# Feed-forward stage 3 of a four-layer block: gate and up products of both token halves interleaved over two banks

## The reference, cut to what matters

```python
def _matmul_lora(x, w, a, b, scale=1.0):
    out = jnp.einsum('bsd,hd->bsh', x, w)
    out = out + jnp.einsum('bsr,hr->bsh', jnp.einsum('bsd,rd->bsr', x, a), b) * scale
    return out
gate = _matmul_lora(x, gate_w, gate_a, gate_b)
up = _matmul_lora(x, up_w, up_a, up_b)
hidden = jax.nn.silu(gate) * up
out = _matmul_lora(hidden, down_w, down_a, down_b)
...
x = x + jnp.tanh(g_ffn[2]) * _L2_ffn_ref(_layernorm(x, axis=-1), ...)
```

## Time and profile before

| | before |
|---|---|
| median of 3 runs (lowest to highest) | 3038.99 us (3037.25 to 3041.05) |
| span of the profiled execution | 3039.3 us |
| TensorE (PE) busy, matmuls | 2869.5 us (94%), 14914 |
| weight loads (PEld) busy | 2371.4 us (78%), 14914 |
| VectorE (DVE) busy | 1945.8 us (64%) |
| ScalarE (ACT) busy | 1097.9 us (36%) |
| GpSimd (POOL) busy | 909.7 us (30%) |
| chain that ended last | PE 81%, DVE 11%, ACT 4%, issue 3% |

### The profile page before, as it was taken

How to read it: one execution, slowest core, us unless ns; L and a number is a source line. 1 busy time by engine, 2 the same in 40 slices (tenths; PEclk the granted TensorE clock), 3 DMA queues, 4 the chain that set the end, 5 groups by cost and what they waited for, 6 DMA issues and landing times.

```text
span 3039.3 us, 47992 instructions
## 1 busy us (share of the span) xinstructions
PE 2869.5 (94%) x14914; PEld 2371.4 (78%) x14914; DVE 1945.8 (64%) x4181; ACT 1097.9 (36%) x3288; POOL 909.7 (30%) x780
## 2 busy tenths in 40 slices
PE   7997799999999999898999999989999999999997
PEld 5665588888888887676888888868877888888886
DVE  5666765565566556575888888854462666666667
ACT  4654233333333333123444444421113444444442
POOL 5433043243334324222222222234442222222210
PEclk9998999999999999999999999999999999999999
DMA  3000011011111111011011101111111001001000
GB/s 128 15 4 18 20 46 40 27 52 38 35 41 41 38 31 46 25 32 35 29 28 32 32 28 28 29 35 52 53 49 45 25 26 29 25 26 29 25 8 28
DMA packets 55235, 104.40 MB, mean 34 GB/s; under 512 B 6672, under 2 KB 6928, under 8 KB 54928
## 3 DMA queue, kind: packets, MB, share of 16 engines
q1 hardware_dynamic: 51840, 94.39, 10.8%
q10 hardware_dynamic: 3216, 7.81, 0.7%
HBM read 100.09 MB, written 2.10 MB: 34 GB/s over the span
## 4 chain that ended last, share of the span: by engine, by line
PE 81%; DVE 11%; ACT 4%; issue 3%; ACTq 0%; DVEq 0%
PE proj L577 35%; PE outp L577 21%; PE score L577 12%; PE value L577 9%; PE turned L806 3%; ACT probs L1231 3%; DVE top L1585 1%; DVE x L1526 1%; DVE stats L1382 1%; DVE probs L1564 1%; DVE probs L1602 1%; DVE xt_lo L1411 1%; DVE sums L1596 0%; DVE probs L1406 0%; DVE vz L1478 0%
## 5 line engine op out<-in xcount | busy, mean ns | idle before, releaser
L526 POOL TENSOR_TENSOR w_hi<-raw,zero 128x512 fp32r<-128x512 f32 x352 | 377.5, 1072 | 1819.2 <-PE proj L577 638.8
L1526 DVE SCALAR_TENSOR_TENSOR x<-outp,gate,x 128x512 f32<-128x512 f32 x800 | 574.4, 744 | 53.8 <-PE outp L577 53.7
L530 POOL TENSOR_TENSOR w_lo<-raw,w_hi 128x512 fp32r<-128x512 f32 x352 | 467.2, 1327 | 27.6
L577 PE MATMUL proj<-xt_hi,w_lo 128*128 128x512 f32 x928 | 396.6, 427 | 9.3 <-DVE xt_lo L1411 4.8
L577 PE MATMUL outp<-w_hi,a_lo 128*128 128x512 f32 x800 | 334.8, 418 | 48.4 <-DVE a_lo L1634 25.2
L577 PE MATMUL proj<-xt_hi,w_hi 128*128 128x512 f32 x928 | 367.9, 396 | 0.0
L577 PE MATMUL proj<-xt_lo,w_hi 128*128 128x512 f32 x928 | 366.1, 394 | 0.0
L577 PE MATMUL outp<-w_hi,a_hi 128*128 128x512 f32 x800 | 317.8, 397 | 0.0
L577 PE MATMUL outp<-w_lo,a_hi 128*128 128x512 f32 x800 | 317.1, 396 | 0.0
L1101 ACT ACTIVATE pT<-turned 128x512 f32<-128x512 f32 x320 | 192.2, 601 | 292.4 <-PE turned L806 292.4
L1602 DVE TENSOR_TENSOR probs<-probs,inv 128x512 f32<-128x512 f32 x320 | 285.8, 893 | 8.8
(11 more groups left out here) (242 smaller groups left out, 5127.9 us busy)
## 6 DMA issues: line engine op xcount, KB each, us to landing
raw<-in_stream SPq DMA_DIRECT2D x352, 256.0 KB, 2.6
ctx_raw<-in_ctx_t ACTq DMA_DIRECT2D x4, 512.0 KB, 6.1
x<-in_x_in ACTq DMA_DIRECT2D x2, 1024.0 KB, 11.7
pb<-in_position_bias ACTq DMA_DIRECT2D x1, 2048.0 KB, 8.8
out<-x SPq DMA_DIRECT2D x8, 256.0 KB, 2.0
qw<-in_qweight ACTq DMA_DIRECT2D x1, 768.0 KB, 4.0
ln_w<-in_ln_weight ACTq DMA_DIRECT2D x1, 256.0 KB, 2.8
q_bi<-in_q_bias ACTq DMA_DIRECT2D x1, 256.0 KB, 2.6
```

Source lines behind the costliest of these rows:

```text
L526: pool.tensor_tensor(w_hi[:, k, :], raw[:, k % RAW, :], zero[:, :].to_broadcast([P, D]), ALU.add)\
L530: pool.tensor_tensor(w_lo[:, k, :], raw[:, k % RAW, :], f32(w_hi[:, k, :]), ALU.subtract)\
L577: m = pe.matmul(out_, l, r, start=start, stop=stop, skip_group_check=True)
L1526: dve.scalar_tensor_tensor(out=x[:, b, :], in0=O[no_f(k) % 2][:, :], scalar=g, in1=x[:, b, :], op0=ALU.mult, op1=ALU.add)\
```

## The change

`gate_or_up` no longer makes one half at a time. It is called with w (gate or up) and part (0 or 1). Each stationary tile is used for half 0 into J[w] and, right after it, for half 1 into S[w]. Part 0 holds the low-rank matmuls and the first two of the four tiles of width (16 matmuls), part 1 the other two (12). The down work is spread over the gaps behind the parts: behind gate part 0 nothing; behind gate part 1 `down_low` and tiles 0, 1, 2; behind up part 0 tiles 3, 4, 5; behind up part 1 tiles 6, 7. ScalarE makes both silus one after the other, VectorE adds tiles 0 to 5 of the down product and then makes `hidden` for both halves, and then adds tiles 6, 7. The number of matmuls, their shapes and operands are the same.

```diff
-                def gate_or_up(j, t, w):
-
-                    no = 2 * j + t
+                def gate_or_up(j, w, part):
+
                     lora, c = f_chunk(2, ("l", j)), f_chunk(2, ("gu"[w], j))
-                    if w == 0 and no >= 2:
-                        pe.wait_ge(s["hid"], no - 1)
-                    if j == 0:
-                        pe.wait_ge(s["low_lo"], t + 1)
-                    dst = (J if t == 0 else S)[w][:, :]
-                    stacked(dst, ring(lora, tokens(w)), M2["low"][:, half(t)], True, True, False)
-                    for kt in range(KT):
-                        last = kt == KT - 1
-                        m = mm3(dst, ring(c, tokens(kt)), acts("x", kt, half(t)), False, last, last)
-                    m.then_inc(s["proj"], 1)
-                    owed[0] += t
+                    dst = J[w][:, :], S[w][:, :]
+                    if part == 0:
+                        if j:
+                            pe.wait_ge(s["hid" if w else "silu"], 2 * j)
+                        else:
+                            pe.wait_ge(s["low_lo"], 2)
+                        for no, rows in enumerate(ring(lora, tokens(w))):
+                            for t in range(2):
+                                told(mm(dst[t], rows, M2["low"][:, half(t)], no == 0, False))
+                    for kt in (0, 1) if part == 0 else (2, 3):
+                        both = ring(c, tokens(kt))
+                        for no, (a, b) in enumerate(((1, 0), (0, 1), (0, 0))):
+                            done = kt == KT - 1 and no == 2
+                            for t in range(2):
+                                m = mm(dst[t], both[a], acts("x", kt, half(t))[b], False, done)
+                                if done:
+                                    m.then_inc(s["proj"], 1)
+                                else:
+                                    told(m)
+                    if w or not j:
+                        owed[0] += part
...
                 for j in range(HIDDEN_TILES):
-                    for no, (t, w) in enumerate(((0, 0), (0, 1), (1, 0), (1, 1))):
-                        gate_or_up(j, t, w)
-
-                        if j and no == 0:
+                    for no in range(4):
+                        gate_or_up(j, no // 2, no % 2)
+
+                        if j and no == 1:
                             down_low(j - 1)
-                        if j:
-                            down(j - 1, range(2 * no, 2 * no + 2))
+                            owed[0] += 1
+                        if j and no:
+                            down(j - 1, range(3 * no - 3, min(3 * no, B)))
...
-                        act.wait_ge(s["proj"], 2 + 2 * no + 1)
+                        act.wait_ge(s["proj"], 2 + 4 * j + t + 1)
...
-                        act.wait_ge(s["hid"], no + 1)
+                    for t in range(2):
+                        act.wait_ge(s["hid"], 2 * j + t + 1)
...
-                    dve.wait_ge(s["proj"], 2 + 2 * no + 2)
+                    dve.wait_ge(s["proj"], 2 + 4 * j + t + 3)
...
                     if j:
-                        add_tiles(j - 1, range(0, 2))
+                        add_tiles(j - 1, range(0, 6))
                     hidden(j, 0)
-                    if j:
-                        add_tiles(j - 1, range(2, 6))
                     hidden(j, 1)
```

## The result

| | before | the change |
|---|---|---|
| median (lowest to highest), 5 runs each | 3038.99 us (3037.25 to 3041.05) | 3052.52 us (3044.12 to 3053.32) |
| ratio | | 1.0035, 95% interval 1.002 to 1.005 |
| profiled execution | span 3039.3 us | time 3052.52 us, span 3049.9 us |
| F2, from its first gate matmul to L3's first matmul | 229.65 us | 239.44 us |
| behind F2, to the last matmul | 771.7 us | 771.3 us |

The change makes the kernel slower: 0.35% by the ratio of the runs, which is 10.6 us, and 13.5 us by the two medians; forecast were 13.3. The two spans differ by 10.6 us. Runs of one kernel scatter with their mean granted clock: of the change's five, the one at 0.988 had a span of 3041.4 us and the one at 0.982 had 3051.4.

A forecast was written before the change was run, and what follows sets the result against it. TensorE, waiting for nothing, was taken to bound F2: number of matmuls times spacing. Terms 1.6 + 8.2 + 1.7 + 1.8 = 13.3 us on the median of 3038.99 gave 3052.3 us, range 3045 to 3061.

The forecast's parts named there:

- Runs of three down tiles: In F2's periods, the third tile waits 0.41 us for VectorE to hand over its bank, 20 times: +8.2 us.
- Weight loads: In F2's gate and up matmuls, loads are already hidden, so using a stationary tile twice saves nothing: 0 us.
- Spacing: In F2's 616 gate and up matmuls, alternating banks gives the down run's 0.2333 us spacing: +1.6 us.
- Start: At j = 0 the first gate matmul must wait for low_lo of both halves: +1.7 us.
- Hidden chain inside the periods: In F2's periods, hidden of both halves starts later but is still ready before down_low needs it: 0 us.
- End: At j = 10 no gate work covers the hidden chain, taken with one slow hid_lo: +1.8 us, bounds 0.7 and 2.9.
- (b): Rival: shared tiles shorten the gate and up spacing, giving back 8.1 us: 3042.6 us, or 3046.7; chance 0.10.
- (c): Rival: faster than before, a tile's second matmul taking 0.173 us or less: 3033 us or less; chance 0.02.
- (d): Rival: the hidden chain becomes the bound, down_low waiting some 1 us in each of 10 periods: 3062 us; chance 0.06.
- (e): Rival: almost no cost, the O bank's hand-over being quicker in a run of three than at the end: 3044 us; chance 0.04.

The follow-up runs named there:

- e1_pairs: The change with down tiles in runs of two instead of three: 3050.84 us against 3041.09 for the kernel before, ratio 1.003.
- e2_threes: The kernel before with only its down tiles regrouped into runs of three, three and two, nothing interleaved: 3046.47 us, ratio 1.0024.
- e3_apart: The change with half 1 taking the width tiles in swapped order, so gate and up tiles are not used twice in a row: 3053.25 us, ratio 1.0037.
- e9_change_placed: The change plus 20 satisfied waits, so that L3's loop starts at instruction 11733 as in the kernel before: 3049.37 us, ratio 1.0029.
- e6_before_placed: The kernel before plus 176 satisfied waits (88 instructions) in F2, so that L3's loop starts at instruction 11821: 3046.34 us, ratio 1.0022.

## Why the prediction was right

The direction, the size and the main mechanism held; one smaller term had the wrong sign. Step by step:

- **Runs of three down tiles, forecast 8.2 us.** Right. The hand-over takes 1.58 us in the change as it did in the last run of before, and 18 loads wait in nine periods. By the periods a run of three costs 0.40 us (20.64 against 19.84 in e1_pairs, for two). e2_threes shows it alone (F2 + 7.9 us) and e1_pairs shows the change without it (F2 - 8.4 us).
- **Weight loads, forecast 0.** Right: e3_apart has the same F2 to 0.1 us with the sharing gone, and the 750 matmuls of the change's window have 749 loads. The Trainium skill (TensorE: Matmul & The Clock Gate, "What happens when you issue a matmul") says that one can load once and matmul repeatedly. No run here did that: each matmul brought its load along, so its gain was not put to the test.
- **Spacing, forecast +1.6 us.** The sign was wrong. With the runs of three gone, in e1_pairs, a period takes 19.84 us, against 19.87 in before: alternating the bank with each matmul costs nothing and rather gains a trifle, 0.3 us in ten periods. The step that failed was to take the down run's 0.2333 as the nearest row since it changes bank often. What makes the down run slower stays open; a change of bank by itself does not, as the interleaved products show (0.2275 to 0.2288 us each).
- **Start, forecast 1.7 us.** Right, in a row against the earlier trace rows:

```profile
2034.67 0.68 DVE L1824 TENSOR_TENSOR low<-score,low 32x512 fp32r<-32x512 f32 x1 [3.10 <-ACT low L1111]
...
2035.50 0.47 PE L577 MATMUL proj<-low,w_hi 128*128 128x512 f32 x1 [1.50 <-DVE low L1824]
```

  VectorE's instruction came 0.41 us earlier in this execution than in before, so the first matmul would have been at 2033.84: 1.66 us, and 0.08 for the longer first matmul.
- **Hidden chain inside the periods, forecast 0.** Right: `turned` waits for `hid_lo` only at the end, and the waits of the nine periods have no such row.
- **End, forecast 1.8 us.** The sum was right, its parts were not. The timeline of the change, against the earlier trace rows:

```profile
2253.20 0.39 PE L577 MATMUL score<-xt_hi,w_hi 128*128 128x512 f32 x1
...
2256.84 1.40 DVE L1837 TENSOR_TENSOR hid_lo<-hid,hid_hi 128x512 fp32r<-128x512 f32 x1 [0.70 <-ACT hid_hi L1111]
...
2258.38 0.77 PE L577 MATMUL value<-hid_hi,w_lo 128*128 128x512 f32 x1 [1.77 <-DVE hid_lo L1837]
...
2262.19 0.50 PE L577 MATMUL outp<-w_hi,hid_lo 128*128 128x512 f32 x1
```

  One `hid_lo` was slow (1.40 us, not 1.80), and `value` came 5.18 us behind the last up matmul, not 5.6, which makes 1.4 us. From there to the third tile it took 3.81 us, where before had 3.33: the granted clock had fallen, which the prediction did not reckon with, and the three `value` matmuls started 0.99 us apart from first to last, not 0.55. The end costs 8.99 - 7.12 = 1.9 us; that the two misses cancel is luck.

Start 1.7, ten periods at 0.78 each 7.8 and end 1.9 make 11.4 us, against 13.3 forecast and 13.5 by the medians; e9_change_placed, with more runs beside it, has 9.6 us. So the terms agree to 2 us, the misjudged spacing being most of the difference, and the match of the forecast with the first pair of medians to 0.2 us is luck. Of the rivals, (b) and (c) are refuted by e3_apart for this program, (d) by the waits, (e) by the hand-over's 1.58 us. What no rival had is the placement of L3's loop: the change itself moved it by 10 instructions only, which the stretch behind F2 does not show (771.3 against 771.7 us).

## What to carry to other kernels

On an engine that is busy all the time, ask first what a new order makes it wait for: here regrouping tiles from two to three on two banks cost 0.4 us twenty times, since the hand-over from a tile to the tile after next takes longer (1.58 us to its second matmul) than the matmuls in that stretch (1.17 us). The price could be read before the change in the one place where the same run already stood. Reusing a tile saves nothing while each matmul still brings a load that is hidden behind the matmul before. And before two orders are compared by the clock of the whole program, compare the stage itself: instructions added to one stage can move a later loop and cost as much as the effect that is looked for.

## What the runs showed of the hardware

- The place of a loop in TensorE's program matters. With L3's loop starting at instruction 11733 (or 11723), the weight loads of its first score matmuls wait about 3 us once at each of the two turns; with the start at 11821 they wait 2.2 to 3.6 us a second time, two matmuls later. e6_before_placed is 6.6 us slower with nothing else changed. That these are waits for instructions is a guess from the profile's "issue", which names no releaser; which placements are good was not tried beyond these three.
- In the change, TensorE idled for 0.70 and 1.77 us at the end of F2, and the granted clock then fell to the lower level (1.2 GHz) for a while:

```profile
2258.00:2262.00 4.00, 3.62 (x9) 2.67 (x9) 3.54 (x6) 0.60 (x1) 2.78 (x3) 0.57 0.40 128
```

  Matmuls started 0.42 us apart there (2258.95, 2259.37, 2259.80), not 0.23. Before idled 1.31 us and then 0.99 us in that place without a fall.
- `hid_lo` on VectorE takes 0.69 us alone. When it starts while a GpSimd split is under way, it ends about 0.55 us after the split, however long that still runs: in the earlier trace rows the split ends at 2147.86 and `hid_lo` at 2148.40, 1.80 us long, and at the end of the change it is 1.40 us long and ends 0.56 us after this split:

```profile
2256.65 1.03 POOL L526 TENSOR_TENSOR w_hi<-raw,zero 128x512 fp32r<-128x512 f32 x1
```

  A `hid_lo` that started 0.10 us before a split ended (at 2254.85) took 0.69 us. `hid`, which reads PSUM, stayed at 0.68 to 0.69 us in every case.
